# A graph-attention and mixture-of-experts kernel: batch 0's early units run before slot 0, and the experts' scatters go out by half blocks

## The reference

```python
q, k, v = (x @ Wq.T), (x @ Wk.T), (x @ Wv.T)           # x: layer-normed, split into 8 heads
scores = einsum('bqhd,bkhd->bhqk', q, k) / sqrt(32)
scores = where(adj != 0, scores, -inf)
c = einsum('bhqk,bkhd->bqhd', softmax(scores), v)
gate = sigmoid(concat([c, x]) @ Wg.T + bg)
x = x_in + gate * x + (1 - gate) * c
...
y = einsum('eni,eih->enh', silu(g) * u, Wd)            # per expert, of layer-normed x
out = x + einsum('ne,enh->nh', cw, y) + silu(flat @ Sg) * (flat @ Su) @ Sd
```

## Time and profile before

| | us |
|---|---|
| median of 3 runs | 1765.62 (1765.43 to 1767.83) |
| the profiled execution, its own time | 1763.22 |
| span of that execution in the trace | 1761.3 |
| PE busy in the span | 1710.9 (97%) |
| DVE busy | 1295.5 (74%) |
| ACT busy | 1087.1 (62%) |
| POOL busy | 647.5 (37%) |

### The profile page before, as it was taken

The page is one execution under the profiler, slowest core; times in us unless marked ns, Lnnn a source line. Parts: engine busy times, 40 slices in busy tenths (PEclk is TensorE's granted clock), DMA queues, the critical chain, the costliest instruction groups (busy, mean ns, idle before and its releaser), DMA issues. The chain is left out here.

```text
span 1761.3 us, 35940 instructions
## 1 busy us (share of the span) xinstructions
PE 1710.9 (97%) x12469; PEld 1449.3 (82%) x12469; DVE 1295.5 (74%) x3217; ACT 1087.1 (62%) x2477; POOL 647.5 (37%) x479
## 2 busy tenths in 40 slices
PE   5999999999999999998999999999999999999996
PEld 4678888778788887786888888889898989898886
DVE  4678888888888888887555655777777777777773
ACT  3998888998988889988433333334434443444342
POOL 0135544444555444444211000043344434343343
PEclk8999999999999999999999999999999999999999
DMA  4555565655555666644333356355565556555653
GB/s 148 137 143 154 167 183 167 175 165 172 168 157 164 184 169 172 173 141 141 121 100 132 102 175 216 121 167 159 138 179 154 158 146 174 151 153 159 168 127 36
DMA packets 140946, 269.19 MB, mean 153 GB/s; under 512 B 15072, under 2 KB 92256, under 8 KB 135776
## 3 DMA queue, kind: packets, MB, share of 16 engines
q1 hardware_dynamic: 113760, 230.45, 42.5%
q0 software_dynamic: 26592, 35.67, 9.9%
q10 hardware_dynamic: 416, 0.79, 0.2%
HBM read 141.99 MB, written 74.52 MB: 123 GB/s over the span
## 5 line engine op out<-in xcount | busy, mean ns | idle before, releaser
L1243 POOL DMA_INDIRECT out_x<-yb,ix x142 | 248.0, 1746 | 558.2 <-ACT yb L1466 457.1
L890 DVE CUSTOM_DVE_ANT_0 pf<-bank,bias_q 128x512 f32<-128x512 f32 x512 | 348.9, 687 | 135.2 <-PE bank L523 131.4
L1478 ACT ACTIVATE ah<-am 128x512 fp32r<-128x512 f32 (+1 forms) x220 | 133.1, 605 | 425.4 <-DVE am L1546 425.4
L655 ACT ACTIVATE pf<-pf,nmax 128x512 f32<-128x512 f32 x512 | 374.2, 731 | 28.7 <-DVE nmax L890 28.2
L1377 PE MATMUL bank<-xh,wh 128*128 128x512 f32 (+1 forms) x880 | 334.8, 381 | 0.9 <-ACT pt L643 0.9
L1378 PE MATMUL bank<-xl,wh 128*128 128x512 f32 (+1 forms) x880 | 334.5, 380 | 0.0
L1379 PE MATMUL bank<-xh,wl 128*128 128x512 f32 (+1 forms) x880 | 334.1, 380 | 0.0
L534 PE MATMUL bank<-ident,pf 128*128 128x128 f32 x2048 | 311.8, 274 | 5.7 <-DVE pt L882 3.6
L534 PEld LDWEIGHTS bank<-ident,pf 128*128 128x128 f32 x2048 | 251.7, 141 | 60.8 <-issue 20.3
L643 ACT ACTIVATE pt<-bank 128x512 f32<-128x512 f32 x480 | 288.5, 601 | 9.3 <-PE bank L534 7.7
L1549 DVE TENSOR_TENSOR al<-am,ah 128x512 fp32r<-128x512 f32 (+1 forms) x220 | 146.8, 667 | 147.6 <-ACT ah L1478 147.6
(11 more groups left out here) (210 smaller groups left out, 3092.0 us busy)
## 6 DMA issues: line engine op xcount, KB each, us to landing
raw<-in_w_all SPq DMA_DIRECT2D x39, 1536.0 KB, 7.0
stack<-qk SPq DMA_DIRECT2D x378, 128.0 KB, 2.4
xb<-xg_dram SPq DMA_DIRECT2D x32, 520.0 KB, 8.0
adj_i<-in_adj SPq DMA_DIRECT2D x32, 512.0 KB, 4.4
xn<-in_x SPq DMA_DIRECT2D x16, 512.0 KB, 6.4
xn_dram<-xn SPq DMA_DIRECT2D x16, 512.0 KB, 2.8
xp<-in_x SPq DMA_DIRECT2D x16, 512.0 KB, 6.7
xnp<-xn_dram SPq DMA_DIRECT2D x16, 512.0 KB, 7.8
```

Source lines behind the costliest of these rows:

```text
L655: act.activation(pf[i][:, :], pf[i][:, :], ACT.Exp, bias=nmax[:, i:i + 1], scale=-1.0, accum_out=den[:, g, tq, j:j + 1]).then_inc(p_exp, 1)
L890: dve.tensor_tensor_reduce(pf[r][:, :], S[p % 2][:, :], bias_q[1 - par][:, tq, :], -SCALE, -3.0 * MASKED, ALU.add, ALU.min, nmax[:, r:r + ...
L1243: pool.indirect_dma_start(out=out, out_offset=bass.IndirectOffsetOnAxis(ap=ix[n % RING][:, i:i + 1], axis=0), in_=yb[s][:, i, :], in_offse ...
L1478: act.activation(ah[s][:, m, 0:cols], am[m % 2][:, 0:cols], ACT.Copy).then_inc(s_ah, 1)
```

## The change

Four things are edited. The units of batch 0 that stand ahead of C0 in the table (L0, M0, Q1, K1, V0, V1, of which the first two are bare semaphore steps in batch 0) leave slots 0 to 9 of batch 0 and run at the end of batch -1 on PE, ACT and DVE. On DVE they stand ahead of `prepare`. All twelve stack transfers go out on SP in the order of the heads. `split_qkv` is called once for each half of the features, and PE waits for the half that it needs; both masks of batch 0 are made later. In the expert phase POOL waits for `s_y[0]` alone before a block's first half of transfers, and for `s_y[1]` before the second.

```diff
+        EARLY = [u for u in ORDER if UNIT_AT[u] < UNIT_AT["C0"]]
...
         def pieces(b, p):
+            if b == 0:
+                return [u for u in PIECES[p] if u[0] not in EARLY]
...
                     if first(b):
-                        refs(B, unit(b, "K0") + 1, range(0, GRP, 2))
+                        refs(B, unit(b, "K0") + 1, range(GRP))
...
                 elif name[0] in "QK":
-                    if first(b) and piece == 0:
-                        pe.wait_ge(s_lo, 2)
+                    if first(b):
+                        pe.wait_ge(s_lo, piece + 1)
...
+                if first(b) and p == POS - 1:
+
+                    par0, att0, pre0, post0 = flags(0)
+                    for name in EARLY:
+                        if has(0, name, att0, pre0, post0):
+                            for piece in range(2):
+                                do_unit(0, par0, name, piece, piece == 1)
+                        else:
+                            pe.wait_ge(g_full, unit(0, name))
+                            pe.nop().then_inc(g_full, 1)
...
                 if first(b) and p == POS - 1:
-                    act.wait_ge(g_free, unit(b, "K0") + 1)
-                    for r in range(1, GRP, 2):
-                        send_head(act, r)
+
+                    par0, att0, pre0, post0 = flags(0)
+                    for name in EARLY:
+                        if has(0, name, att0, pre0, post0):
+                            if name[0] != "V":
+                                evacuate(0, par0, name)
+                        else:
+                            pass_by(0, name)
...
-                scores_mask(-1, 0, 0)
...
-                    if p == UNIT_AT["P0"] + 1:
-                        split_qkv()
+                    if p in (UNIT_AT["P0"] + 1, UNIT_AT["P0"] + 2):
+                        split_qkv(p - UNIT_AT["P0"] - 1)
                     if p == UNIT_AT["P1"] + 2:
+                        scores_mask(b, par, 0)
+                    if p == END_AT["K0"] + 3:
                         scores_mask(b, par, 1)
-                    if p == END_AT["K0"] + 3:
+                    if p == POS - 1:
+
+                        par0, att0, pre0, post0 = flags(0)
+                        for name in EARLY:
+                            if has(0, name, att0, pre0, post0):
+                                low(0, par0, name)
                         prepare()
...
             def add(n, s, first):
 
-                for j in range(2):
-                    pool.wait_ge(s_y[j], n + 1)
+                pool.wait_ge(s_y[0], n + 1)
...
                 for i in range(tiles(n)):
+                    if i == tiles(n) // 2:
+                        pool.wait_ge(s_y[1], n + 1)
+                        pool.nop().then_inc(s_held_pool, 1)
                     pool.indirect_dma_start(
```

More of the change, by code:

```diff
@@ L312, in f32, with done @@
             return t.bitcast(F32)
+        def done(b, p):
+            return [u for u in DONE.get(p, []) if b != 0 or u not in EARLY]
         def first(b):
@@ L606, in evacuate, with pass_by @@
                                    ACT.Copy).then_inc(g_free, 1)
+            def pass_by(b, name):
+                act.wait_ge(g_full, unit(b, name) + 1)
+                if name in HI:
+                    act.wait_ge(g_hi, hi_index(b, name))
+                else:
+                    act.wait_ge(g_free, unit(b, name))
+                act.nop().then_inc(g_hi if name in HI else g_free, 1)
             def second_choice(A):
@@ L621, in at @@
                     act.activation(wg_h[:, :, :], x1[:, :, :], ACT.Copy).then_inc(s_set, 1)
-                for name in ["L0"] if b > NB and p == 0 else [] if b > NB and p == 1 else DONE.get(p - 1, []):
+                for name in ["L0"] if b > NB and p == 0 else [] if b > NB and p == 1 else done(b, p - 1):
                     if name[0] in "RVX":
@@ L627, in at @@
                     else:
[L629 to L634, removed]
+                        pass_by(b, name)
                 eb, ep, was = behind(b, p, EVAC, att)
@@ L681, in vector, with split_qkv @@
             dve.memset(rw_wide[:, :, :], 0.0).then_inc(s_pick, 1)
[L683 to L687, removed]
+            def split_qkv(k):
+                dve.wait_ge(s_set, 2 + k)
+                dve.tensor_tensor(wqkv_l[:, k, :], (df if k else zf)[:, 0:3 * D], f32(wqkv_h[:, k, :]),
+                                  ALU.subtract).then_inc(s_lo, 1)
             def prepare():
@@ L892, in at @@
                                              nmax[:, r:r + 1]).then_inc(s_done, 1)
-                for name in DONE.get(p - 2, []):
+                for name in done(b, p - 2):
                     if name[0] in "PQKC" and has(b, name, att, pre, post):
@@ L897, in at @@
                         skip(b, name)
-                for name in DONE.get(p - 1, []):
+                for name in done(b, p - 1):
                     if name[0] in "VX" and has(b, name, att, pre, post):
```

## The result

The changed kernel takes 1756.58 us (median of 5 runs, 1756.1 to 1758.93) against 1765.62 of before: 9.0 us less, ratio 0.995 with a 95% interval from 0.9939 to 0.9961. Measured again later, beside other runs of before, it took 1757.77 against 1765.2 (7.4 us less, 0.9957, 0.9944 to 0.9971). The profiled execution took 1757.09, with a span of 1755.4. That is 6.1 us less than the profiled execution of before, so the first pair of traces shows only part of the 9.0; the experiments come back to that.

What follows compares the result with a forecast made beforehand. PE, busy 97% of the span, bounds the kernel, so only its waits at both ends can be won: 1.6 us at the start and 2.7 at the end make 4.3, giving 1761.3 us, range 1757.2 to 1764.4 (low clock's milder end).

Steps and rivals of the forecast that it cites:

- What is won at the start is kept: Start of the kernel: time gained there reaches the total, since PE runs without slack behind it.
- the 0.9 us for the earlier K0: K0's output at the start: moved mask and split halves gain between 0 and 1.7 us, taken as 0.9.
- I take about 5 us at 1.2 GHz and the rest at 2.4 ... end 28.5.: Early units on PE from 20.6: eleven of twelve large matmuls in 5 us, the rest in 2.9.
- the clock stays up: Rival at the start: the pause before Q1 keeps 2.4 GHz, early units end at 26.0, total 1758.0; chance 0.2.
- First pass, slot 12, P0: DVE's first pass at 32.0, slot 12's pass at 44.2, P0 of the next batch at 53.7, not 55.30.
- the 0.8: First pass to slot 12: added for tiles and transposes coming later after PE's idle and clock fall; bound 2.1.
- the start, forecast at 1.6: Gain of the whole start, read at P0 of the next batch: 53.7 in place of 55.30.
- Cost the path nothing: Twelve stack transfers on one queue, 19.7 to 28.2: slot 0 does not come before 28.5, so no cost.
- head 0's gain: Stack transfers in head order on one queue: head 0 can only be earlier than 25.8, while slot 0 waits until 28.5.
- 2.7 forecast: End of the kernel: scatters of the last full block start earlier, gaining 2.7 us, with 1.7 as lower bound.
- The wait in the middle: Rival at the end: it costs POOL 0.79 instead of 0.31 per block, end worth 1.7, total 1762.3; chance 0.1.
- The rival of the scatters beside DVE's conversions: Expert phase: earlier scatters hold up weight conversions in 39 routed blocks and PE waits, total 1769.1; chance 0.03.

Runs made afterwards that it cites:

- a2: The changed kernel, unchanged, measured and profiled once more: 1757.77 us, ratio 0.9957 to the kernel before.
- a3: The changed kernel, unchanged, profiled a third time: 1757.63 us in one run, beside 1765.23 for the kernel before.
- e6: The changed kernel with one more wait on PE, holding the early units until head 0 is in the stack: 1763.5 us, ratio 0.9989 to before.
- e3: The changed kernel with the stack transfers of heads 1 and 3 on ACT's queue again, ahead of the early units' outputs: 1762.67 us, ratio 0.9984 to before.
- e4: The changed kernel with an empty list of early units, so Q1, K1, V0, V1 run in slots 2 to 9 again: 1760.21 us, ratio 0.9968 to before.
- e1: The kernel before with the half-block scatters at the end alone: 1763.38 us, ratio 0.9986 to before.
- e5: The changed kernel with `prepare` cut into five steps spread over slots 6 to 26 of batch 0: 1757.88 us, ratio 0.9958 to before.

## Why the prediction was right or wrong

**The bound.** Right in the expert phase. "What is won at the start is kept" was too simple: P0 to slot 36 took between 24.10 and 26.72 us over the versions, following the low stretch and the length of the issues, so a gain at P0 is only part of what one execution shows.

**K0 and Q1.** The low part of K0 ended at 19.7, as forecast. Q1 started at 19.95 and not 20.6: the second mask, 0.69 us, does not stand in its way, since Q1 began while it ran (19.64 to 20.32). That is 0.65 us. In a2 and a3 Q1 started earlier still, at 19.17 and 18.60: the clock rose there at 16.68 and 15.71, while K0 ran, and not at 18.73. So the 0.9 us for the earlier K0 were too little as well; the first stack issue puts it at about 1.4.

**The early units, the step that failed.** "I take about 5 us at 1.2 GHz and the rest at 2.4 ... end 28.5." They ran at 2.4 GHz throughout, 5.75 us, and ended at 25.7; the pause of 1.59 us cost no clock, and in a2 and a3 (1.60 us) neither. Against the forecast of 7.9 us that is 2.15 us. e6 shows the case that the prediction had taken for likely, with a pause of 5.47 us. The rival "the clock stays up" was right there, and its chance of 0.2 too little. The forecast expected a pause of about 2.3 us and judged it by what the one of 7.50 in the earlier trace rows had cost; no row showed what a short one costs.

**First pass, slot 12, P0.** From the end of the early units to the first pass 3.5 us were forecast and 3.74 measured; from there to slot 12's pass 12.2 and 12.31, with the clock at 1.2 GHz from 28.97 to 35.80; then 9.5 and 9.48. These three steps came out in size. Whether the 0.8 in them was the clock's price is not shown: in a2 and a3 the low stretch was half as long (3.41 us) and the step to slot 12 hardly shorter, 12.06 and 12.21. So P0's 51.23 in place of 53.7 is 0.65 and 2.15, less 0.33: the start, forecast at 1.6, was worth 4.1 in this pair and 4.5 on the means.

**The transfers.** "Cost the path nothing" was right for the changed kernel. What the prediction passed over is the queue that they leave: ACT's, which e3 puts at 4.66 us at P0. It also took head 0's gain for hidden; it is, behind the early units, but e4 shows that without them most of P0's move would have come from the small edits alone; of these the forecast priced only the earlier K0, at 0.9.

**The end.** 2.7 forecast, 2.7 (e1) and 2.8 (traces) measured. The wait in the middle cost POOL nothing (0.30), so that rival falls. The rival of the scatters beside DVE's conversions shows nowhere: PE was busy for 896.63 of 897 us.

**The sum.** 4.5 and 2.8 on the median of before would be 1758.3. Measured were 1756.58 and 1757.77. So of the 4.7 us between 1761.3 and the first median, 2.9 are the start, most of it the early units' clock, and 0.1 the tail. The rest, 1.7 us (0.5 for the second median), is of the size by which medians of the same kernel differed between measurements (1765.2 to 1766.1 for before, 1.2 us for after); 0.6 of it lies on the means between P0 and slot 36, and it stays without a cause shown. The upper end of the range, 1764.4, is 0.2 above the sum that it names (1764.2); nothing hangs on that.

## What to carry to other kernels

When work is moved into a wait, price what the pause ahead of it will be after the change and not what it was before: here 1.59 us cost no clock, and 3.34 (e3) and 5.47 (e6) did. Try issuing transfers that one consumer wants in order from one queue in that order, and not from an engine whose next result is waited for: here the first tile started 3.87 us behind the issue and not 6.12, and ACT was free 5.07 us sooner. Before a few us are read out of one pair of traces, take two or three of each kernel, and count from an event near the edit and not from the start of the span: the span of one trace of before lay 1.9 and 3.5 us under those of the two others.

## What was not expected of the hardware

The twelve issues of 128 KB on SP's queue, the same instructions at the same place of the program, took from 7.67 to 9.53 us (7.67 to 8.96 in three traces of the unchanged after), and PE waited for heads up to 1.29 us in e5 behind the longest. On ACT's queue six took 5.07 us in which ACT did nothing else. PE's clock rose while or just after K0 ran, at 15.71 to 18.73 us in three traces of one kernel, and Q1's start differed by 1.35 us with it. And the same wait of 1.04 us ahead of P0 was followed by a stretch at 1.2 GHz in one of three traces of the changed kernel and not in the other two.
